# Mamba scan in a metaformer block: a chunk's skip added by TensorE and written by ScalarE instead of VectorE

## The chip, the cores and the metric

One core of a Trainium2 chip runs the whole program. The metric is the device time of one execution in microseconds (us); less is better.

## The reference, cut to what matters

Two metaformer blocks on `x` of 4 samples, 256 channels, 1024 positions. The first block's mixer is a Mamba layer on four chunks of 64 channels; it is the part that the change touches:

```python
h = exp(dt * A) * h + (dt * x) * B          # 16 states, a scan over 1024 positions
y = sum_s h[s] * C[s]                       # read-out
y = (y + xc * D_param) * silu(z)
ym = einsum('bld,od->blo', y, out_proj_w)   # 128 -> 64 channels
ym = ym + skip_scale * chunks               # the skip: chunks is the layer's scaled input
```

The rest (layer norms, an fp8 linear layer, channel attention, a mixture of 8 experts) is left as it is.

## The kernel before, in words

The program has a front (about 0 to 1165 us: four samples, one after the other, then the last sample's later layers) and a mixture-of-experts part. In the front each sample has a stretch of scans, with 64 steps `i` = 16 states `s` for each of the 4 chunks `c`. Every engine runs its own list of instructions in the order in which the code issues them, and they meet at semaphores. Nothing is planned while it runs, so an instruction that waits holds up all that is behind it on its engine.

What a step does:

- ScalarE, `decay(i)` (L1138): exp of 128x1024, into PSUM banks 0-1 or 2-3, or into SBUF for the steps whose drive comes through TensorE. It waits until scan `i-2` is done. Then come `scale_blocks(i)` (L1160, 2 to 4 small products that prepare the next such "turned" drive) and some small work for the next sample (L869, `first_sum`).
- GpSimd, `drive(i)` (L1246) for the steps that aren't turned, and the read-outs `h * C` of 34 of the 64 steps (`read_out`, L1257, two steps late). At step 39 of a sample it also runs one tiny `first_shift` (L1228), which waits for a tiny VectorE reciprocal (L1310, `first_small`) that stands behind VectorE's read-out of step 37.
- VectorE, `scan(i)` (L1567) and the other 30 read-outs (L1577) from the row of C that TensorE spread into banks 4-5 (`crep`).
- TensorE, `turned_drive` (L477, 8 transposes), `c_row` (the row of C, bf16, into banks 4-5), and `sum_states(i-1)` (adds the product of a step into banks 6-7, `ysum`). Its helper has one line for all matrix products, L474.

At the start of chunk `c` (step 16c+1), the chunk before is closed: VectorE multiplies `ysum` by silu(z) (`gate`, L1605, into YF), TensorE projects YF (`out_proj`) into banks 2-3, which the odd decays use too, and VectorE adds the scaled input and writes the chunk into YM (`skip`, L1610). TensorE's next chunk of sums starts with `direct` (the D_param term, two products), which waits for the gate. ScalarE's decay of the step with s = 3 waits for the skip, as it writes banks 2-3. The last chunk of a sample has a path of its own (L1589, L1597).

```python
if c and s == 3:
    act.wait_ge(ym_done, b * NC + c)          # decay, L1136-1137
```

In chunks 1 to 3 the steps with s = 2, 3 and 4 are read out by GpSimd, those with s = 1 and 5 by VectorE, so banks 4-5 hold no row of C in between.

Of the kernel before, what the change touches and what calls it, by code (L numbers as in the profile page):

```python
# [10 lines left out]
ALU = mybir.AluOpType  # L11
# [3 lines left out]
P = 128  # L15
# [4 lines left out]
NC = 4  # L20
# [117 lines left out]
def build_front(nc, t, out, xm_rows, bc_rows, logits, routing, experts):  # L138
    with ExitStack() as ctx:
# [149 lines left out]

        DECAY_SB = XC[:, 0, :]  # L290
        B_TOK = ffn_w.rearrange("p c o -> p (c o)").rearrange("p (n c k) -> p n c k", n=NB, c=NC)

        def square_tile(c):
            return H[:, c % 2, :]
# [177 lines left out]
        def _(pe):  # L472
            def mm(o, lhsT, rhs, start, stop, **k):
                return nc.tensor.matmul(o, lhsT, rhs, start=start, stop=stop, **k)  # L474
# [288 lines left out]
            def scans(b):  # L763
                pe.wait_ge(sz_done, (b + 1) * NC * NH)
                def read_done(i):
                    if on_pool(i):
                        pe.wait_ge(pool_read, b * pool_reads(NI) + pool_reads(i + 1))
                    else:
                        pe.wait_ge(dve_read, b * dve_reads(NI) + dve_reads(i + 1))

                def c_row(i):
                    c, s = i // NS, i % NS
                    if on_pool(i):
                        return
                    if last_on_dve(i - 1) >= 0:
                        pe.wait_ge(dve_read, b * dve_reads(NI) + dve_reads(i))
                    if on_pool(i - 1) and i - 1 in TOK_AT:
                        pe.wait_ge(tok_copied, b * (NC + 1) + (TOK_AT.index(i - 1) + 2))
                    for h in range(NH):
                        m = mm(psum[:, 4 + h, :], sel[:, s, :], BCS[:, c, h * HL:(h + 1) * HL], True, True)  # L780
                    m.then_inc(crep_ready, 1)

                def dtx_turn(c):

                    i = TOK_AT[c]
                    assert on_pool(i) and not on_pool(i + 1)
                    pe.wait_ge(dtx_done, b * NC + c + 1)
                    pe.wait_ge(dve_read, b * dve_reads(NI) + dve_reads(i))
                    for n in range(NB):
                        m = turn(psum[:, 4 + n // 4, (n % 4) * P:(n % 4 + 1) * P], DTX[:, c, n * P:(n + 1) * P])  # L790
                    m.then_inc(tok_turned, 1)

                def turned_drive(i):
                    c, k = i // NS, i % 2
                    pe.wait_ge(h_ready, b * NI + (i - 1))
                    pe.wait_ge(scaled, b * turned_drives(NI) + turned_drives(i) + 1)
                    for n in range(NB):
                        m = turn(psum[:, 2 * k + n // 4, (n % 4) * P:(n % 4 + 1) * P], scaled_tile(c)[:, n, :])
                    m.then_inc(turned_ready, 1)

                def direct(c):
                    if c:
                        pe.wait_ge(yf_ready, b * NC + c)
                    for h in range(NH):
                        mm(psum[:, 6 + h, :], diag_d[:, :], XC[:, c, h * HL:(h + 1) * HL], True, False,
                           skip_group_check=True)

                def sum_states(i):
                    read_done(i)
                    for h in range(NH):  # L810
                        m = mm(psum[:, 6 + h, :], ident[:, :], PRODUCT[PRODUCT_IN[i]][:, h * HL:(h + 1) * HL], False,
                               i % NS == NS - 1, skip_group_check=True)
                        if i == NI - 1 and h == 0:
                            m.then_inc(ysum_half, 1)
                    m.then_inc(ysum_done, 1)

                def out_proj(c):
                    i = min((c + 1) * NS + 1, NI - 1)
                    pe.wait_ge(h_ready, b * NI + (i + 1))
                    p0 = DM * (c % 2)  # L820
                    for h in range(NH):
                        if c == NC - 1 and h == 0:
                            pe.wait_ge(yf_half, b + 1)
                        else:
                            pe.wait_ge(yf_ready, b * NC + c + 1)
                        m = mm(psum[p0:p0 + DM, 2 + h, :], outp_w[:, :], YF[:, h * HL:(h + 1) * HL], True, True)
                        if c == NC - 1 and h == 0:
                            m.then_inc(op_half, 1)
                    m.then_inc(op_ready, 1)

                pe.wait_ge(bc_spread, b * (3 * NC * 16) + 3 * NC * 16)
                c_row(0)
                direct(0)
                for i in range(1, NI):
                    c = i // NS
                    if i % NS == 1 and c:
                        out_proj(c - 1)
                    if i + 2 < NI and is_turned(i + 2):
                        turned_drive(i + 2)
                    if i in TOK_AT:  # L840
                        dtx_turn(TOK_AT.index(i))
                    c_row(i)
                    if i % NS == 1 and c:
                        direct(c)
                    sum_states(i - 1)
                sum_states(NI - 1)
                pe.wait_ge(dve_read, b * dve_reads(NI) + dve_reads(NI))
                xhat_turn(b + 1, 0)
                out_proj(NC - 1)
                xhat_turn(b + 1, 1)  # L850
                y_turn(b)

# [10 lines left out]
        def _(act):  # L863
# [261 lines left out]
            def scans(b, after):  # L1125
                def decay(i):
                    c, s = i // NS, i % NS
                    if i == 0 and after:
                        act.wait_ge(xmt_done, b * 2)
                    if i == 1 and after:  # L1130
                        act.wait_ge(gate_done, b)
                    if s == 0:
                        act.wait_ge(dt_done, b * NC + c + 1)
                    if i >= 2:
                        act.wait_ge(h_ready, b * NI + (i - 1))
                    if c and s == 3:  # L1136
                        act.wait_ge(ym_done, b * NC + c)
                    nc.scalar.activation(DECAY_SB if is_turned(i) else decays[i % 2], DT[:, c, :], ACT.Exp, scale=a_neg[:, s:s + 1]).then_inc(da_ready, 1)  # L1138

                def dtx_tokens(c):  # L1140
                    act.wait_ge(tok_turned, b * (NC + 1) + (c + 2))
# [24 lines left out]
                for i in range(NI):  # L1166
                    decay(i)
                    if i - 2 == TOK_AT[0]:
                        dtx_tokens(0)
                    scale_blocks(i)  # L1170
                    if i - 2 in TOK_AT[1:]:
                        dtx_tokens(TOK_AT.index(i - 2))
                    if 4 <= i < 8 and after:
                        last_norm(b - 1, (2 * i - 8, 2 * i - 7))
                    n = (i - FIRST_AT) % NB
                    k = (i - FIRST_AT) // NB
                    if k == 0:
                        first_sum(b + 1, n)
                    if k == 1:
                        if n == 0:  # L1180
                            first_mean(b + 1)
                        first_square(b + 1, n)
                    if k == 2 and n == 0:
                        first_std(b + 1)
                    if k == 3:
                        first_norm(b + 1, n)
# [98 lines left out]
        def _(dve):  # L1285
# [264 lines left out]
            def scans(b):  # L1550
# [53 lines left out]
                        dve.wait_ge(op_ready, b * NC + c)  # L1604
                    v.tensor_tensor(halves(YF), ysum, halves(SZ[:, c, :]), ALU.mult).then_inc(yf_ready, 1)  # L1605

                def skip(c):
                    dve.wait_ge(op_ready, b * NC + c + 1)
                    p0 = DM * (c % 2)
                    v.scalar_tensor_tensor(halves(YM[p0:p0 + DM, c // 2, :]), halves(xn[p0:p0 + DM, c // 2, :]),  # L1610
                                           scal[p0:p0 + DM, 0:1], op[p0:p0 + DM, :, :], ALU.mult,
                                           ALU.add).then_inc(ym_done, 1)

                for i in range(NI):
                    c, s = i // NS, i % NS
                    scan(i)
                    if c and s == 1:
                        gate(c - 1)
                    if c and s == 2:
                        skip(c - 1)  # L1620
                    if i:
                        read_out(i - 1)
                    if i == FIRST_AT + 2 * NB + NB // 2:
# [51 lines left out]
            for d in range(CT):  # L1675
# [3 lines left out]
                                 ALU.subtract))  # L1679
            fold(v.tensor_tensor(gate_w[:, :, :], gate_w[:, :, :], psum[:, 2, C:C + E].unsqueeze(1).broadcast_to((P, CT, E)),  # L1680
                                 ALU.subtract))
            assert folds[0] == FOLD_DVE
            for c in range(NC):
                log1p(0, c)
# [5 lines left out]


PREP_EPS, PREP_DVE, PREP_ALL = 6, 11, 11 + 3 + 2 + 6 + 5 + 1
FOLD_NBR, FOLD_WG, FOLD_DVE = 12, 14, 20
FIRST_AT = 18
TOKENS_AT, NEXT_AT, X_AT, LAST_DT_AT = 12, 15, 36, 9

# [496 lines left out]
```

## Time and profile before

| | |
|---|---|
| median of 3 runs | 1836.05 us (1835.17 to 1837.93) |
| the profiled execution's own time | 1832.81 us |
| its span | 1830.9 us |
| busy: TensorE, GpSimd, VectorE, ScalarE | 1564.3, 1074.1, 1158.7, 1002.1 us |

The profile is of one execution. Busy shares are means over stages with different limits: in the scans GpSimd and VectorE are both nearly full, in the expert part TensorE is. Times in the rows are us from the start of the span, unless marked ns.

### The profile page before, as it was taken

To read this page: it belongs to the slowest core of one execution; us is meant where nothing else is said; L and a number is where in the kernel's file an instruction comes from. 1 tells how busy PE (TensorE), PEld (TensorE's weight loads), DVE (VectorE), ACT (ScalarE), POOL (GpSimd) and SP (SyncE) were. 2 spreads that over 40 slices of the span, in tenths; PEclk is the share of its full clock that TensorE was granted. 3 is DMA by queue.
4 is the path that set the end of the run, shared out by engine and by line. 5 is a ranking of instruction groups with operands and counts; after the bars stand their busy time and mean duration, and the time that the engine had idled before them with its cause. 6 is when DMAs were issued, how large, how long until landed. Compare 5 with 4: busy or idle time off the path is not lost. (4 is left out here: it accounts for less than half of the span.)

```text
span 1830.9 us, 22984 instructions
## 1 busy us (share of the span) xinstructions
PE 1564.3 (85%) x6577; PEld 1012.4 (55%) x6578; DVE 1158.7 (63%) x1344; ACT 1002.1 (55%) x1950; POOL 1074.1 (59%) x574
## 2 busy tenths in 40 slices
PE   5589889979888888888898888673599999999997
PEld 2144435644444553443564444452488888888896
DVE  3399998489997579998758999746522222222222
ACT  6768775878874887885687877321122222222222
POOL 0499991279995158999037999300345555455543
PEclk9799999999999999999998999895699999999999
DMA  3356650156762055765026676642022222222222
GB/s 104 99 185 228 221 197 10 50 184 224 241 203 86 1 170 196 248 204 169 2 78 217 195 240 200 247 179 71 25 36 34 37 37 39 35 34 40 34 33 26
DMA packets 78401, 222.43 MB, mean 121 GB/s; under 512 B 12588, under 2 KB 31349, under 8 KB 74966
## 3 DMA queue, kind: packets, MB, share of 16 engines
q1 hardware_dynamic: 62390, 202.54, 32.8%
q0 software_dynamic: 15904, 18.66, 6.6%
q8 instruction: 43, 0.70, 0.2%
q14 instruction: 64, 0.52, 0.1%
HBM read 199.76 MB, written 19.82 MB: 120 GB/s over the span
## 5 line engine op out<-in xcount | busy, mean ns | idle before, releaser
L474 PE MATMUL psum<-HC_sb,ident_sb 128*128 128x512 f32 x768 | 368.4, 606 | 36.1 <-POOL HC_sb L1257 25.5
L1986 ACT ACTIVATE hgt_sb<-psum_moe,b_sb 128x256 f32<-128x256 f32 (+1 forms) x312 | 116.5, 456 | 379.8 <-PE psum_moe L1893 252.0
L474 PE MATMUL psum<-experts_sb 64*128 64x512 f32 (+5 forms) x834 | 258.4, 551 | 70.6 <-DVE HC_sb L1577 18.8
L1893 PE MATMUL psum_moe<-XGT_sb,w1s_sb 128*128 128x256 f32 (+1 forms) x1248 | 254.9, 363 | 0.0
L2138 DVE TENSOR_TENSOR YS_sb<-psum_moe,b_sb 128x256 f32<-128x256 f32 x71 | 30.1, 424 | 352.8 <-PE psum_moe L1893 349.2
L1893 PE MATMUL psum_moe<-experts_sb,hgt_sb 128*128 x1136 | 251.7, 379 | 0.7 <-DVE YS_sb L2138 0.7
L1870 POOL DMA_INDIRECT out<-YS_sb,scat_sb x71 | 128.3, 1806 | 209.5 <-DVE YS_sb L2142 193.1
L1138 ACT ACTIVATE psum<-experts_sb 128x1024 f32<-128x1024 f32 x168 | 186.1, 1108 | 118.2 <-DVE experts_sb L1567 70.5
L474 PEld LDWEIGHTS psum<-HC_sb,ident_sb 128*128 128x128 f32 x768 | 139.8, 191 | 189.3 <-issue 104.6
L1160 ACT ACTIVATE experts_sb<-experts_sb 128x128 f32<-128x128 f32 x704 | 227.7, 388 | 18.4 <-PE psum L477 15.2
L1893 PEld LDWEIGHTS psum_moe<-XGT_sb,w1s_sb 128*128 128x128 f32 x1248 | 219.5, 192 | 25.5
L1893 PEld LDWEIGHTS psum_moe<-experts_sb,hgt_sb 128*128 128x128 f32 x1136 | 215.2, 190 | 30.1 <-issue 1.1
L1567 DVE TENSOR_TENSOR_SCAN experts_sb<-psum,DBX_sb 128x1024 f32<-128x1024 f32 x92 | 209.0, 2278 | 27.4 <-ACT psum L1138 13.7
L474 PEld LDWEIGHTS psum<-experts_sb 64*128 64x128 f32 (+5 forms) x834 | 88.5, 155 | 212.3 <-issue 138.1
L1567 DVE TENSOR_TENSOR_SCAN experts_sb<-experts_sb,psum 128x1024 f32<-128x1024 f32 x88 | 199.9, 2272 | 1.9 <-ACT experts_sb L1138 1.4
L1209 POOL TENSOR_TENSOR experts_sb<-experts_sb 128x1024 f32<-128x1024 f32 x16 | 38.7, 2416 | 261.0 <-DVE XSUM_sb L1453 182.8
L1257 POOL TENSOR_TENSOR HC_sb<-X_XT_sb,experts_sb 128x1024 f32<-128x1024 f32 x76 | 180.0, 2372 | 10.7 <-DVE experts_sb L1567 8.2
L1858 POOL DMA_INDIRECT XG_sb<-xm_rows,tab_sb x71 | 70.7, 996 | 163.6 <-DMA gate_rows<-p21t_sb 142.3
L477 PEld LDWEIGHTS psum<-ident_sb,experts_sb 128*128 128x128 f32 x864 | 96.4, 142 | 103.9 <-ACT experts_sb L1160 49.5
L477 PE MATMUL psum<-ident_sb,experts_sb 128*128 128x128 f32 x864 | 114.8, 278 | 31.7 <-ACT experts_sb L1160 14.6
L474 PE MATMUL psum<-experts_sb,ident_sb 128*128 128x512 f32 x256 | 122.9, 602 | 15.1 <-POOL experts_sb L1257 13.4
L1577 DVE TENSOR_TENSOR HC_sb<-psum,experts_sb 128x1024 f32<-128x1024 f32 x96 | 115.3, 1201 | 2.4 <-PE psum L474 2.2
(298 smaller groups left out, 2381.0 us busy)
## 6 DMA issues: line engine op xcount, KB each, us to landing
X_XT_sb<-bc_rows SPq DMA_DIRECT2D x116, 512.0 KB, 4.1
DA_sb<-bc_rows SPq DMA_DIRECT2D x88, 512.0 KB, 5.2
experts_sb<-bc_rows SPq DMA_DIRECT2D x40, 512.0 KB, 5.4
SQ_sb<-bc_rows SPq DMA_DIRECT2D x40, 512.0 KB, 5.9
T_sb<-bc_rows SPq DMA_DIRECT2D x20, 512.0 KB, 5.5
experts_sb<-w1T SPq DMA_DIRECT2D x8, 1024.0 KB, 19.8
experts_sb<-w2T SPq DMA_DIRECT2D x8, 1024.0 KB, 21.8
X_sb<-x_tok SPq DMA_DIRECT2D x5, 1024.0 KB, 6.9
```

Of the source, the lines that this page charges most:

```text
L474: return nc.tensor.matmul(o, lhsT, rhs, start=start, stop=stop, **k)
L477: return nc.tensor.transpose(o, src, ident[:, :])
L1138: nc.scalar.activation(DECAY_SB if is_turned(i) else decays[i % 2], DT[:, c, :], ACT.Exp, scale=a_neg[:, s:s + 1]).then_inc(da_ready, 1)
L1160: m = nc.scalar.activation(scaled_tile(c)[:, n, :], DTX_TOK[:, n, :], ACT.Copy, scale=B_TOK[:, n, c, j % NS:j % NS + 1])
L1209: nc.gpsimd.tensor_tensor(DT[:, c, :], DTX[:, c, :], log_tile(c), ALU.add).then_inc(dt_done, 1)
L1257: nc.gpsimd.tensor_tensor(PRODUCT[PRODUCT_IN[i]], c_rep(q), STATE[STATE_IN[i]], ALU.mult).then_inc(pool_read, 1)
L1567: v.tensor_tensor_scan(STATE[STATE_IN[i]], decay, drive, 0.0, ALU.mult, ALU.add).then_inc(h_ready, 1)
L1577: v.tensor_tensor(halves(PRODUCT[PRODUCT_IN[i]]), crep, halves(STATE[STATE_IN[i]]), ALU.mult).then_inc(dve_read, 1)
L1858: pool.indirect_dma_start(XG[:, k, :], None, xm_rows, bass.IndirectOffsetOnAxis(ap=TAB[:, tile:tile + 1], axis=0)).then_inc(xg_ready[k], 16)
L1870: pool.indirect_dma_start(out, bass.IndirectOffsetOnAxis(ap=SCAT[:, tile:tile + 1], axis=0), YS[:, tile % 4, :], None, compute_op=ALU.add) ...
L1893: return nc.tensor.matmul(o, lhsT, rhs, start=start, stop=stop, **k)
L1986: m = nc.scalar.activation(HGT[:, k, 4 * h + q, 0:w], psum[:, 2 * h + q // 2, (q % 2) * 2 * P:(q % 2) * 2 * P + w], ACT.Gelu, bias=b1[:, b ...
```

## The change

The scaled input is added on TensorE: a 64-row diagonal `SKIP` (skip_scale on the diagonal, both halves of the partitions) times the chunk's input, accumulated behind the projection. Both go into banks 4-5, in the gap between the read-outs of s = 1 and s = 5, one half (512 positions) at a time: the first after the sum of step 16c+1, the second after the sum of step 16c+2. ScalarE copies the result into YM at s = 5. VectorE's skip is gone, the wait moves from ScalarE's decay (s = 3) to TensorE's row of C (s = 5), and `SKIP` is built once at the start by two small VectorE instructions. The last chunk of a sample is as before.

```diff
@@ c_row
+                    if c and s == 5:
+                        pe.wait_ge(ym_done, b * NC + c)
@@ TensorE, the projection
-                def out_proj(c):
-                    i = min((c + 1) * NS + 1, NI - 1)
-                    pe.wait_ge(h_ready, b * NI + (i + 1))
-                    p0 = DM * (c % 2)
+                def out_proj(c, h):
+                    i, p0 = (c + 1) * NS + 1, DM * (c % 2)
+                    pe.wait_ge(yf_ready, b * NC + c + 1)
+                    pe.wait_ge(dve_read, b * dve_reads(NI) + dve_reads(i + 1))
+                    at = psum[p0:p0 + DM, 4 + h, :]
+                    mm(at, outp_w[:, :], YF[:, h * HL:(h + 1) * HL], True, False)
+                    m = mm(at, SKIP[p0:p0 + DM, :], xn[p0:p0 + DM, c // 2, h * HL:(h + 1) * HL], False, True)
+                    if h:
+                        m.then_inc(op_ready, 1)
@@ TensorE, the loop over steps
-                    if i % NS == 1 and c:
-                        out_proj(c - 1)
                     if i + 2 < NI and is_turned(i + 2):
                         turned_drive(i + 2)
...
                     sum_states(i - 1)
+                    if c and i % NS in (2, 3):
+                        out_proj(c - 1, i % NS - 2)
@@ ScalarE
-                    if c and s == 3:
-                        act.wait_ge(ym_done, b * NC + c)
+                def chunk_out(c):
+                    act.wait_ge(op_ready, b * NC + c + 1)
+                    p0 = DM * (c % 2)
+                    nc.scalar.activation(halves(YM[p0:p0 + DM, c // 2, :]), crep[p0:p0 + DM, :, :], ACT.Copy).then_inc(ym_done, 1)
...
                     scale_blocks(i)
+                    if i >= NS and i % NS == 5:
+                        chunk_out(i // NS - 1)
@@ VectorE
-                def skip(c):
-                    dve.wait_ge(op_ready, b * NC + c + 1)
-                    p0 = DM * (c % 2)
-                    v.scalar_tensor_tensor(halves(YM[p0:p0 + DM, c // 2, :]), halves(xn[p0:p0 + DM, c // 2, :]),
-                                           scal[p0:p0 + DM, 0:1], op[p0:p0 + DM, :, :], ALU.mult,
-                                           ALU.add).then_inc(ym_done, 1)
...
-                    if c and s == 2:
-                        skip(c - 1)
@@ VectorE, once at the start
+            fold(v.tensor_tensor(SKIP, ident[:, 0:DM], ident[:, DM:P], ALU.add))
+            fold(v.tensor_scalar(SKIP, SKIP, scal[:, 0:1], None, ALU.mult))
```

## Rows read from the trace of the kernel before

**Rows 1.** The page: groups by line; the line VectorE's skip has.

```profile
L1610 DVE SCALAR_TENSOR_TENSOR T_sb<-experts_sb,scal_sb,psum 64x1024 f32<-64x1024 f32 x12 | 15.1, 1259 | 0.1
```

**Rows 2.** Who waited for whom, ScalarE: us in total, times, longest.

```profile
ACT psum L1138 <- DVE T_sb L1610: 46.9, 8, 6.3
```

**Rows 3.** Busy time by stretch (PE, PEld, DVE, ACT, POOL; clock, DMA share), second sample.

```profile
433.90:481.10 47.20, 42.25 (x140) 19.75 (x140) 44.71 (x25) 39.76 (x97) 46.24 (x21) 1.00 0.65 213
481.10:531.85 50.75, 42.54 (x142) 19.93 (x142) 46.33 (x27) 39.16 (x76) 47.84 (x25) 1.00 0.65 221
```

**Rows 4.** GpSimd in order of time: start, duration, then idle time before it.

```profile
437.51 2.36 POOL L1257 TENSOR_TENSOR experts_sb<-X_XT_sb,experts_sb 128x1024 f32<-128x1024 f32 x1 [0.82 <-DVE experts_sb L1567]
...
456.25 2.36 POOL L1257 TENSOR_TENSOR experts_sb<-X_XT_sb,experts_sb 128x1024 f32<-128x1024 f32 x1
...
490.86 2.36 POOL L1257 TENSOR_TENSOR HC_sb<-X_XT_sb,experts_sb 128x1024 f32<-128x1024 f32 x1 [1.19 <-DVE experts_sb L1567]
...
498.71 0.21 POOL L1228 TENSOR_TENSOR experts_sb<-experts_sb 128x8 f32<-128x8 f32 x1 [0.84 <-DVE experts_sb L1310]
...
554.70 2.39 POOL L1257 TENSOR_TENSOR HC_sb<-X_XT_sb,experts_sb 128x1024 f32<-128x1024 f32 x1
```

**Rows 5.** GpSimd's waits in chunk 2 of the first sample (189.1 to 240.1).

```profile
POOL HC_sb L1257 <- DVE experts_sb L1567: 2.1, 2, 1.5
POOL experts_sb L1228 <- DVE experts_sb L1310: 1.2, 1, 1.2
```

**Rows 6.** The same of the fourth sample (1067.7 to 1118.4).

```profile
POOL HC_sb L1257 <- DVE experts_sb L1567: 2.0, 2, 1.3
```

**Rows 7.** TensorE's products in order of time, start of chunk 1, second sample.

```profile
435.24 4.16 PE L474 MATMUL psum<-experts_sb 128*64 128x512 f32 x10 [1.42 <-DVE experts_sb L1605]
...
440.95 1.04 PE L477 MATMUL psum<-ident_sb,experts_sb 128*128 128x128 f32 x8
441.82 1.88 PE L474 MATMUL psum<-HC_sb,ident_sb 128*128 128x512 f32 x4
443.54 1.88 PE L474 MATMUL psum<-experts_sb,ident_sb 128*128 128x512 f32 x4
```

**Rows 8.** TensorE's weight loads: the front's start (64-row tiles), then chunk 1.

```profile
43.37 0.19 PEld L474 LDWEIGHTS psum<-experts_sb 64*128 64x128 f32 x2 [0.24 <-issue]
...
436.12 0.14 PEld L474 LDWEIGHTS psum<-experts_sb 128*64 128x64 f32 x1 [0.29 <-issue]
437.07 0.64 PEld L474 LDWEIGHTS psum<-experts_sb 128*128 128x128 bf16 x4 [0.81 <-issue]
```

**Rows 9.** ScalarE in order of time, chunk 1 of the second sample.

```profile
445.81 0.40 ACT L869 ACTIVATE X_sb<-X_sb 128x256 f32<-128x256 f32 x1
...
446.21 1.13 ACT L1138 ACTIVATE experts_sb<-experts_sb 128x1024 f32<-128x1024 f32 x1
```

**Rows 10.** One line's instructions: ScalarE's copy of PSUM into SBUF (min/median/max ns).

```profile
L1144 ACT ACTIVATE experts_sb<-psum x16: 1024/1024/1025, 97.8 to 1105.7; 128x1024 f32<-128x1024 f32 x16
```

**Rows 11.** VectorE in order of time, around the three chunk starts of the second sample.

```profile
433.89 1.20 DVE L1605 TENSOR_TENSOR experts_sb<-psum,experts_sb 128x1024 f32<-128x1024 f32 x1
...
447.47 2.29 DVE L1567 TENSOR_TENSOR_SCAN experts_sb<-experts_sb,psum 128x1024 f32<-128x1024 f32 x1 [0.35 <-ACT experts_sb L1138]
...
452.98 2.26 DVE L1567 TENSOR_TENSOR_SCAN experts_sb<-psum,experts_sb 128x1024 f32<-128x1024 f32 x1
...
481.13 1.22 DVE L1605 TENSOR_TENSOR experts_sb<-psum,experts_sb 128x1024 f32<-128x1024 f32 x1
...
495.12 2.29 DVE L1567 TENSOR_TENSOR_SCAN experts_sb<-experts_sb,psum 128x1024 f32<-128x1024 f32 x1
...
531.85 1.22 DVE L1605 TENSOR_TENSOR experts_sb<-psum,experts_sb 128x1024 f32<-128x1024 f32 x1 [0.48 <-PE psum L474]
...
544.68 2.29 DVE L1567 TENSOR_TENSOR_SCAN experts_sb<-experts_sb,psum 128x1024 f32<-128x1024 f32 x1
```

**Rows 12.** GpSimd's first drive in the order of time.

```profile
83.28 4.64 POOL L1246 TENSOR_TENSOR DBX_sb<-DA_sb,experts_sb 128x1024 f32<-128x1024 f32 x2 [17.96 <-DMA DA_sb<-bc_rows]
```

More of the change, by code:

```diff
@@ L291, in build_front @@
         B_TOK = ffn_w.rearrange("p c o -> p (c o)").rearrange("p (n c k) -> p n c k", n=NB, c=NC)
+        SKIP = FB[:, 0:DM]
         def square_tile(c):
@@ L815, in sum_states, with last_out_proj @@
                     m.then_inc(ysum_done, 1)
-                def out_proj(c):
-                    i = min((c + 1) * NS + 1, NI - 1)
-                    pe.wait_ge(h_ready, b * NI + (i + 1))
-                    p0 = DM * (c % 2)
+                def out_proj(c, h):
+                    i, p0 = (c + 1) * NS + 1, DM * (c % 2)
+                    assert not on_pool(i) and all(on_pool(i + k) for k in (1, 2, 3)) and not on_pool(i + 4)
+                    pe.wait_ge(yf_ready, b * NC + c + 1)
[5 more added lines that the diff above has]
+                        m.then_inc(op_ready, 1)
+                def last_out_proj():
+                    c, p0 = NC - 1, DM * ((NC - 1) % 2)
+                    pe.wait_ge(h_ready, b * NI + NI)
                     for h in range(NH):
-                        if c == NC - 1 and h == 0:
+                        if h == 0:
                             pe.wait_ge(yf_half, b + 1)
@@ L825, in out_proj @@
                             pe.wait_ge(yf_ready, b * NC + c + 1)
[L826 to L829, printed above, removed]
+                        mm(psum[p0:p0 + DM, 2 + h, :], outp_w[:, :], YF[:, h * HL:(h + 1) * HL], True,
+                           True).then_inc(op_ready if h else op_half, 1)
                 pe.wait_ge(bc_spread, b * (3 * NC * 16) + 3 * NC * 16)
@@ L848, in scans @@
                 xhat_turn(b + 1, 0)
-                out_proj(NC - 1)
+                last_out_proj()
                 xhat_turn(b + 1, 1)
@@ L1692 @@
 PREP_EPS, PREP_DVE, PREP_ALL = 6, 11, 11 + 3 + 2 + 6 + 5 + 1
-FOLD_NBR, FOLD_WG, FOLD_DVE = 12, 14, 20
+FOLD_NBR, FOLD_WG, FOLD_DVE = 12, 14, 22
 FIRST_AT = 18
```

## The prediction, made before the changed kernel ran

> **What bounds the kernel now.** I read the busy time by stretch first, then each engine in order of time around the three places per sample where a chunk is closed, then the waits. In the scans of the second sample GpSimd is busy 46.24 of 47.20 us in chunk 1 and 47.84 of 50.75 us in chunk 2, at TensorE's full clock (granted 1.00, the 2.4 GHz level) [rows 3]. So GpSimd sets the pace of chunks 1 to 3; VectorE is late only near a chunk's start. GpSimd's idle time there has names: 0.82 us for scan 18, and in chunk 2 1.19 us for scan 35 and 0.84 us for VectorE's tiny reciprocal [rows 4]; in the first sample the last two are 1.5 and 1.2 us, in the fourth 1.3 us and again the 0.8 us [rows 5, 6]. What happens to VectorE's or ScalarE's time counts only as far as it moves these GpSimd instructions.
>
> The removed pieces: VectorE's skip, 12 times 1.26 us, 15.1 us [rows 1]; ScalarE's waits for it, 46.9 us in the eight of its waits whose decay goes to PSUM [rows 2]. Neither is a gain as it stands.
>
> **What the skip's removal could give.** If nothing new is late, decay 35 runs early, scan 35 follows VectorE's read-out of step 33 at once, and GpSimd's two idle times of chunk 2 close: 2.7 us in the first sample (1.5 + 1.2), 2.0 in the second (1.19 + 0.84), 2.1 in the fourth (1.3 + 0.8), and as much in the third by the same pattern, 9 us in all. In chunk 1 nothing: the 0.82 us stands ahead of the skip, and after it GpSimd is full. In chunk 3 nothing either.
>
> **What the new chain costs.** Count from g, the gate's start; a wait that moves to step s = 5 is only harmless if the copy is ready by then. TensorE works in order, and by row the prices are: four passes of 512 columns (the two products of a state's sum) 1.72 us (441.82 to 443.54), a turned drive 0.87 us (440.95 to 441.82), the last pass's tail 0.16 us (1.88 less 1.72), the first product after the gate at g + 1.35 (435.24 less 433.89) [rows 7, 11]. In the new order there stand behind the gate:
> direct 1.72, the sum of s = 0 1.72, the turned drive of s = 4 0.87, the sum of s = 1 1.72, first half of the projection 1.72 (projection and skip, two passes each), the sum of s = 2 1.72, second half 1.72. With 1.35 that is g + 12.54. After the 64-column passes the next weights stand at 437.07, where 436.12 + 2 x 0.43 is 436.98 [rows 8]: 0.09 per change, 0.18 for two. With the tail: the result is there at g + 12.9. Its inputs are not later than this queue: VectorE's read-out of s = 1 is over near g + 4.4, GpSimd's of s = 2 at 437.51 + 2.36, g + 6.0 [rows 4].
>
> The new products are the skip's, 64 rows by 64 columns, which the trace doesn't show. From below they cost 0 (if they ran beside the projection), by the nearest row, the 128x64 passes, 0.43 us a pass as for full ones [rows 8]; from above I allow the same and 0.25 to 0.5 us more per half for changing shapes twice. I take 0.43 us: time goes by the 512 columns, in all rows.
>
> At this place a rule of the Trainium skill is worth weighing. The row first: on 64-row tiles two weight loads fall into one slot of 0.43 us in the front's start (x2, 0.19 + 0.24 idle) [rows 8], so pairs on disjoint tiles do overlap. The Trainium skill, "TensorEngine Tiling (Array Packing)", Theoretical Speedup, gives up to 2x for a small dimension, and Key Properties says that a change of mode drains the array. By the first the skip's products would be free, by the second both halves dearer. Here projection and skip share their 64 columns and the projection takes all rows, so I expect no overlap.
>
> ScalarE reaches the copy (after decay and scale blocks of s = 5) before that: by my walk through its list near g + 10, and surely before g + 12.3, where decay 22 stood in the old order (446.21) [rows 9]. So it waits about 3 us for TensorE, and the decay of s = 6 is behind it. The copy takes 1.02 us by the PSUM copy of the same length [rows 10]; 64 partitions instead of 128 change nothing I would count on.
>
> *Chunk 1.* Copy g + 12.95, a first_sum behind it (0.40, 445.81 to 446.21), decay 22 from g + 14.3 to g + 15.45 (1.13) [rows 9], scan 22 at g + 15.5. Before: g + 13.58 (447.47). It is 1.9 us later although it had waited for the skip before. From scan 22 VectorE is full up to scan 24 (452.98 less 447.47 is two scans of 2.19 and a read-out of 1.12), so scan 24 starts at g + 21.0 and ends at g + 23.2 [rows 11]. GpSimd's read-out 24 stood at 456.25, g + 22.36, with 1.0 us to spare [rows 4]; it becomes g + 23.3: **+0.9**. Later scans have more to spare.
>
> *Chunk 2.* No first_sum stands here: decay 38 g + 13.95 to g + 15.1, scan 38 at g + 15.1; before at 495.12, g + 13.99 [rows 11]. Its read-out 37, the reciprocal and GpSimd's first_shift follow it without a gap, and GpSimd is idle there already: **+1.1**. The 1.19 us before read-out 35 is gained, and lost again at first_shift. In the first sample both idle times are 0.3 us longer [rows 5], scan 38 is that much later already, and I take +0.8.
>
> *Chunk 3.* Decay 54 at the same g + 13.95, scan 54 at g + 15.1, before 544.68 less 531.85, g + 12.83: 2.2 later [rows 11]. VectorE's scan 56 ends 7.7 us later (three scans, a read-out), g + 22.8; GpSimd's read-out 56 stood at 554.70, g + 22.85 [rows 4]: **0 to +0.1**. The wait is paid from VectorE's slack.
>
> **Edits at nothing.** The two small instructions that build SKIP delay VectorE by some tenths at the start; GpSimd's first drive waits 17.96 us for a DMA there, long after its own work [rows 12]. Without that cover 0.4 us once. TensorE's wait for ym_done before the row of C of s = 5: the copy ends at g + 14, and what is behind it (that row, then the sum of s = 4, which needs GpSimd's product) is wanted only when VectorE has ended the scan of s = 6, g + 17.7. Clearing banks 2-3 for the odd decays gives ScalarE an early decay 19, 35 and 51, which is what exposes the later wait. DMA queues see no new or moved issue; their waits follow GpSimd.
>
> **Sum.** First sample 0.9 + 0.8 = 1.7, the other three 2.0 each plus up to 0.1: 7.7 to 8, I say **+8 us**. On the profiled execution (1830.9 span, 1.9 around it) that is 1840.8; the median of the runs stands 3.2 above that execution, so 1836.05 + 8 = **1844 us**.
>
> **Rivals.**
> 1. The result is ready when ScalarE comes (TensorE's queue is shorter than I make it): GpSimd's idle times of chunk 2 close, -9, 1827 us. For it: the old skip was a wait of over 5 us. Against: seven items of TensorE in a row, each with a measured price, and back-to-back rows. It would need g + 10. Chance 0.12.
> 2. The skip's products overlap with others or cost nearly nothing: the result comes 1.72 earlier, at g + 11.2. Chunk 1: scan 22 +0.2, inside the spare time, 0. Chunk 2: scan 38 0.6 earlier, and so is first_shift, 0.9 in the first sample. -2.7, 1833.4 us, no change to be told. The case of the first rule above. Chance 0.13.
> 3. Forecast, 1844 us: TensorE's queue makes the copy late, the copy holds decay s = 6, that holds VectorE, that holds GpSimd. Decides from about g + 11.8 on (sum zero). Chance 0.60.
> 4. Changes of tile shape drain: 0.25 to 0.5 us more per half, 0.5 to 1 us on all three places, chunk 3 without spare time now: 12 x 0.5 to 12 x 1, 1850 to 1856 us. Chance 0.12. The case of the second rule.
>
> The remaining 0.03 is for VectorE being the bound after all, up to the 15 us of the skip.
>
> **How the numbers follow.** What can be told from no change is 0.2%, 3.7 us. Faster: rival 1 and a little of the rest, 0.15; same: rival 2, and the forecast half-sized, 0.14; slower: 0.71. The range reaches from below rival 2 to the cheaper end of rival 4: 1831 to 1851; outside are rival 1 and the dear end of 4. The forecast's own range is 1840 to 1848.
>
> **What would show it.** ScalarE's new copy idle about 3 us before each of 12, released by TensorE; VectorE idle 4 to 4.6 us before the scans 22, 38 and 54, released by ScalarE's decay; these scans at g + 15.5, 15.1, 15.1; the projection's end at g + 12.9; GpSimd without idle time at read-out 35 but with 3 us at first_shift. Wrong would be: the copy not waiting, the products under 1.72 us per half, or scan 22 at less than g + 14.5.

## The result and the profile after

The changed kernel takes 1849.93 us (median of 4 runs, 1848.79 to 1851.0) against 1836.74 us for the kernel before (4 runs): ratio 1.0075, 95% interval 1.0061 to 1.0089. That is slower, by 13.2 us (11 to 16). The forecast was 1844 us in a range of 1831 to 1851: the direction and the way it happens held, the size was 8 us against 13.

The two profiled executions are further apart, 1848.1 against 1830.9 us of span: the one of the kernel before was 3.9 us faster than that kernel's median, the one of the changed kernel stood at its own. In what follows "gate + x" is x us after the start of VectorE's gate of that chunk. Busy time by stretch says where: here chunk 1, chunk 2 and chunk 3 (up to the last chunk's own path) of the second sample, with the columns of [rows 3].

```profile
437.28:486.25 48.97, 44.34 (x145) 20.04 (x144) 43.04 (x24) 40.92 (x98) 46.27 (x21) 1.00 0.58 207
486.25:538.84 52.59, 44.99 (x147) 20.13 (x146) 44.82 (x27) 40.66 (x78) 47.75 (x25) 1.00 0.62 213
538.84:584.80 45.96, 41.57 (x127) 18.15 (x126) 38.95 (x22) 25.42 (x49) 41.45 (x18) 1.00 0.49 166
```

The stretches were 47.20 and 50.75 us [rows 3], and the third:

```profile
531.85:577.04 45.19, 39.05 (x123) 18.13 (x124) 40.49 (x23) 24.92 (x48) 41.46 (x18) 1.00 0.51 171
```

So +1.8, +1.8 and +0.8 us, at an unchanged clock and with GpSimd's busy time unchanged to 0.1 us. GpSimd has only become idle for longer. VectorE is 1.5 to 1.7 us less busy per chunk and the stretch is longer all the same. The other samples show much the same (first: +1.7, +1.5, +0.7). Four samples give 17 us, as far as the two profiled executions are apart.

GpSimd in order of time (start, duration, idle before), after; against [rows 4]:

```profile
455.72 2.36 POOL L1276 TENSOR_TENSOR HC_sb<-X_XT_sb,experts_sb 128x1024 f32<-128x1024 f32 x1 [0.92 <-DVE experts_sb L1586]
...
461.36 2.36 POOL L1276 TENSOR_TENSOR experts_sb<-X_XT_sb,experts_sb 128x1024 f32<-128x1024 f32 x1 [0.97 <-DVE experts_sb L1586]
...
494.60 2.35 POOL L1276 TENSOR_TENSOR HC_sb<-X_XT_sb,experts_sb 128x1024 f32<-128x1024 f32 x1
...
505.68 0.20 POOL L1247 TENSOR_TENSOR experts_sb<-experts_sb 128x8 f32<-128x8 f32 x1 [4.11 <-DVE experts_sb L1329]
...
562.48 2.36 POOL L1276 TENSOR_TENSOR HC_sb<-X_XT_sb,experts_sb 128x1024 f32<-128x1024 f32 x1 [0.76 <-DVE experts_sb L1586]
```

Read-outs 22 and 24 now wait for VectorE (24 is at gate + 24.1, it was at + 22.4). Read-out 35 has lost its idle time, as the removed skip promised. But first_shift waits 4.11 us where it waited 0.84, and read-out 56 of chunk 3, which had nothing to spare, waits 0.76.

VectorE, after; against [rows 11] (L1624 is the gate):

```profile
437.28 1.19 DVE L1624 TENSOR_TENSOR experts_sb<-psum,experts_sb 128x1024 f32<-128x1024 f32 x1
...
446.08 2.26 DVE L1586 TENSOR_TENSOR_SCAN experts_sb<-psum,DBX_sb 128x1024 f32<-128x1024 f32 x1
453.35 2.29 DVE L1586 TENSOR_TENSOR_SCAN experts_sb<-experts_sb,psum 128x1024 f32<-128x1024 f32 x1 [5.01 <-ACT experts_sb L1150]
...
461.05 1.20 DVE L1596 TENSOR_TENSOR HC_sb<-psum,experts_sb 128x1024 f32<-128x1024 f32 x1
...
502.09 2.29 DVE L1586 TENSOR_TENSOR_SCAN experts_sb<-experts_sb,psum 128x1024 f32<-128x1024 f32 x1 [4.75 <-ACT experts_sb L1150]
...
554.54 2.29 DVE L1586 TENSOR_TENSOR_SCAN experts_sb<-experts_sb,psum 128x1024 f32<-128x1024 f32 x1 [4.36 <-ACT experts_sb L1150]
```

Scans 22, 38 and 54 start at gate + 16.1, + 15.8 and + 15.7, each released by ScalarE's decay. Up to scan 21 VectorE is ahead of the kernel before by 2.1 us (+ 8.8 against + 10.9); then it loses more than that in one wait. ScalarE and who held it:

```profile
450.78 1.02 ACT L1155 ACTIVATE T_sb<-psum 64x1024 f32<-64x1024 f32 x1 [3.75 <-PE psum L477]
451.70 0.40 ACT L883 ACTIVATE X_sb<-X_sb 128x256 f32<-128x256 f32 x1
...
452.10 1.14 ACT L1150 ACTIVATE experts_sb<-experts_sb 128x1024 f32<-128x1024 f32 x1
```

```profile
ACT T_sb L1155 <- PE psum L477: 48.2, 12, 4.2
```

All twelve copies wait for TensorE, about 4 us each, 48.2 us in all. In the kernel before, ScalarE waited twelve times for the skip too: the eight waits of [rows 2], 46.9 us, and four of chunk 2, where a table load stands ahead of the decay and has a row of its own:

```profile
ACT L1138 <- DVE T_sb L1610: 15.1, 4, 3.9
```

That is 62.0 us before and 48.2 after. The wait is a quarter shorter, but it has been moved to where the next turned step needs ScalarE, and there it costs. TensorE's queue, weight loads and products:

```profile
444.75 0.19 PEld L477 LDWEIGHTS psum<-experts_sb 128*64 128x64 f32 x2 [0.76 <-issue]
445.75 0.19 PEld L477 LDWEIGHTS psum<-experts_sb 64*64 64x64 f32 x2 [0.81 <-issue]
446.75 0.30 PEld L477 LDWEIGHTS psum<-experts_sb,ident_sb 128*128 128x128 f32 x2 [0.81 <-issue]
...
448.67 0.19 PEld L477 LDWEIGHTS psum<-experts_sb 128*64 128x64 f32 x2 [0.76 <-issue]
449.67 0.19 PEld L477 LDWEIGHTS psum<-experts_sb 64*64 64x64 f32 x2 [0.81 <-issue]
```

```profile
438.53 1.98 PE L477 MATMUL psum<-experts_sb 128*128 128x512 f32 x4 [0.89 <-DVE experts_sb L1624]
440.35 1.88 PE L477 MATMUL psum<-HC_sb,ident_sb 128*128 128x512 f32 x4
442.07 1.04 PE L480 MATMUL psum<-ident_sb,experts_sb 128*128 128x128 f32 x8
442.94 1.88 PE L477 MATMUL psum<-HC_sb,ident_sb 128*128 128x512 f32 x4
```

The queue is the one forecast, item by item: direct at + 1.25, the sum of s = 0 at + 3.1, the turned drive at + 4.8, the sum of s = 1 at + 5.7, the halves at + 7.5 and + 11.4. Two passes of the projection take from 444.75 to 445.75, two of the skip to 446.75, the sum to 448.67. Without a change of tile shape these would be 0.86, 0.86 and 1.72: the changes in these three stretches add 0.14, 0.14 and 0.20 us, as the weight load no longer runs ahead of the passes before it (0.76 to 0.81 us idle instead of 0.24). From the sum of s = 1 (442.94, gate + 5.66) to the last product (449.67, gate + 12.39) 14 passes take 6.73 us, where 14 x 0.43 is 6.02: the five changes together add 0.71 us.

### The profile page after: what moved, and what is told of

It reads as the page before. It is cut to its first block and busy times, and to the rows that moved or that the text cites. A ratio compares the mean times of both kernels' runs of the same rounds, so it can differ in the third digit from the quotient of the medians.

```text
span 1848.1 us, 23085 instructions
## 1 busy us (share of the span) xinstructions
PE 1589.7 (86%) x6625; PEld 1012.6 (55%) x6626; DVE 1140.4 (62%) x1334; ACT 1014.0 (55%) x1962; POOL 1076.7 (58%) x574
## 5 line engine op out<-in xcount | busy, mean ns | idle before, releaser
L477 PE MATMUL psum<-HC_sb,ident_sb 128*128 128x512 f32 x768 | 372.8, 611 | 35.2 <-POOL HC_sb L1276 18.3
L477 PE MATMUL psum<-experts_sb 64*128 64x512 f32 (+6 forms) x882 | 287.9, 555 | 67.8 <-DVE HC_sb L1596 22.7
L477 PEld LDWEIGHTS psum<-experts_sb 64*128 64x128 f32 (+6 forms) x882 | 90.9, 152 | 230.9 <-issue 138.2
L480 PEld LDWEIGHTS psum<-ident_sb,experts_sb 128*128 128x128 f32 x864 | 96.0, 141 | 100.5 <-ACT experts_sb L1177 40.4
L480 PE MATMUL psum<-ident_sb,experts_sb 128*128 128x128 f32 x864 | 114.1, 277 | 28.7 <-DVE experts_sb L1586 13.7
```

Of the source, the lines that this page charges most:

```text
L480: return nc.tensor.transpose(o, src, ident[:, :])
```

## The experiments

The runs outside the scans vary by a few us from one execution to the next, so each verdict rests on the stretches of the second sample too (chunk 1 and 2 from gate to gate, chunk 3 up to the last chunk's own path). Of "theory" below: TensorE's result is late, and the wait goes over ScalarE and VectorE to GpSimd. The kernel before had a median of 1835.2 to 1835.4 us beside these runs.

| kernel | median us | ratio to before, 95% interval | chunk 1 / 2 / 3, us |
|---|---|---|---|
| before | 1836.74 (beside the change) | | 47.2 / 50.7 / 45.2 |
| the change | 1849.93 | 1.0075 (1.0061, 1.0089) | 49.0 / 52.6 / 46.0 |
| copy_later | 1837.85 | 1.0014 (1.0001, 1.0026) | 47.4 / 51.3 / 45.2 |
| halves_together | 1836.51 | 1.0009 (1.0, 1.0018) | 47.3 / 51.1 / 45.1 |
| no_skip_product | 1832.65 | 0.9986 (0.9977, 0.9995) | 47.4 / 50.6 / 45.1 |
| later_together | 1838.01 | 1.0013 (1.0005, 1.0022) | 47.3 / 51.2 / 45.1 |
| full_rows | 1849.1 | 1.0072 (1.0059, 1.0085) | 48.7 / 52.3 / 45.7 |
| short_copy | 1846.68 | 1.0066 (1.005, 1.0082) | 48.1 / 51.7 / 45.2 |
| before_recip_early | 1830.94 | 0.9983 (0.9971, 0.9996) | 47.3 / 49.8 / 45.2 |
| after_recip_early | 1837.75 | 1.0011 (1.0003, 1.002) | 49.0 / 49.2 / 46.0 |
| spread | 1832.2 | 0.9981 (0.9969, 0.9994) | 47.0 / 49.6 / 45.2 |
| halves_recip_early | 1824.83 | 0.9945 (0.9931, 0.9958) | 47.3 / 48.4 / 45.2 |
| spread_recip_early | 1821.23 | 0.9925 (0.9911, 0.9939) | 47.0 / 48.4 / 45.2 |

**Does the wait cost, or the work?** copy_later only moves the copy:

```diff
                     decay(i)
+                    if i >= NS and i % NS == 6:
+                        chunk_out(i // NS - 1)
...
-                    if i >= NS and i % NS == 5:
-                        chunk_out(i // NS - 1)
```

> The changed kernel with ScalarE's copy moved one decay later: behind decay of s = 6 instead of ahead of it. Theory (the copy waits for TensorE's result at gate + 13.4 and holds decay s = 6, and so scans 22, 38 and 54, and through them GpSimd): scan s = 6 at gate + 11 to 11.5 instead of + 16, the copy still begins at + 13.4 to 13.5, VectorE now waits under 2.5 us for the row of C of s = 5, first_shift about 1 us earlier than in the kernel before: some 4 us under the kernel before, 1832. Rival A (the copy's 1 us of ScalarE work is the price, wherever it stands): no change against the changed kernel, 1850. Rival B (TensorE's added products and shape changes slow the state sums, which hold GpSimd): 1848 to 1850.

The same work, 12 us less than the change: rivals A and B fall as the whole cause. But the median missed the forecast 1832 by 6 us, and chunks 1 and 2 are 0.2 and 0.6 us longer than in the kernel before. Scan 22 did not start at + 11; it started at gate + 14.5 (gate at 433.50), released by TensorE's transposes (L480) and no longer by ScalarE:

```profile
448.03 2.29 DVE L1586 TENSOR_TENSOR_SCAN experts_sb<-experts_sb,psum 128x1024 f32<-128x1024 f32 x1 [3.46 <-PE psum L480]
```

halves_together removes no work either:

```diff
-                    if c and i % NS in (2, 3):
-                        out_proj(c - 1, i % NS - 2)
+                    if c and i % NS == 2:
+                        out_proj(c - 1, 0)
+                        out_proj(c - 1, 1)
```

> The changed kernel with both halves of the projection behind the sum of s = 1, the sum of s = 2 after them. TensorE's work is the same, the result is there some 1.9 us earlier, gate + 11.5. Theory: scan s = 6 at gate + 14.1 (chunk 1) and + 13.9 (chunk 2), against + 13.6 and + 14.0 in the kernel before, so GpSimd loses nothing in chunk 1 and 2: about the kernel before, 1834 to 1839. Rival A: 1850. Rival B: 1850 or more.

The median is as forecast: a result 2 us earlier wins nearly all of the loss back. The scans come a little later than forecast, at gate + 14.4 for + 14.1 and + 13.9, and here too TensorE's transposes release scan 22 (gate at 435.02). ScalarE's decay 22 is over at 449.07, 0.3 us earlier:

```profile
449.40 2.29 DVE L1587 TENSOR_TENSOR_SCAN experts_sb<-experts_sb,psum 128x1024 f32<-128x1024 f32 x1 [3.31 <-PE psum L480]
```

no_skip_product takes the work away:

```diff
-                    mm(at, outp_w[:, :], YF[:, h * HL:(h + 1) * HL], True, False)
-                    m = mm(at, SKIP[p0:p0 + DM, :], xn[p0:p0 + DM, c // 2, h * HL:(h + 1) * HL], False, True)
+                    m = mm(at, outp_w[:, :], YF[:, h * HL:(h + 1) * HL], True, True)
```

> Leaves out the product that adds the scaled input in chunks 0 to 2 (the output lacks it); projection, copy, waits and order as in the changed kernel. It takes two passes and one change of tile shape, 1.0 us, from each half. Theory: result at gate + 11.5, the same times as halves_together, 1834 to 1839. Rival A: 1850, since the copy is there. Rival B: 1836 to 1840 too, as TensorE's added work is gone; it differs from the theory in halves_together only.

The stretches are those of the theory (scan 38 at gate + 13.8, forecast + 13.9); the median is 1 us under the range. Here ScalarE's decay releases the scan, as in the change. Order and work thus buy nearly the same, scan 22 at gate + 14.4 and + 14.1, though what holds it last differs: the queue up to the transposes in the one, the result and the copy in the other.

**The second wait under the first.** later_together has both edits.

> Both edits at once: the copy behind decay s = 6, both halves behind the sum of s = 1. Theory: nothing is late any more: scan s = 6 at gate + 11, row of C of s = 5 ready near + 13.2, when VectorE has just ended that scan; GpSimd's idle time before read-out 35 and first_shift closes: 9 us under the kernel before, 1827 to 1829. Rival A: 1850 less little. Rival B: 1845 to 1850.

A miss by 9 us: no faster than either edit alone. VectorE of this kernel, second sample (gate at 435.93), then TensorE:

```profile
450.30 2.29 DVE L1587 TENSOR_TENSOR_SCAN experts_sb<-experts_sb,psum 128x1024 f32<-128x1024 f32 x1 [3.31 <-PE psum L480]
```

```profile
447.41 1.98 PE L477 MATMUL psum<-experts_sb,ident_sb 128*128 128x512 f32 x4
449.23 1.04 PE L480 MATMUL psum<-ident_sb,experts_sb 128*128 128x128 f32 x8
```

Scan 22 is a turned step, and its drive (the eight transposes at 449.23) stands in TensorE's queue behind both halves and the sum of s = 2. With ScalarE free, the same queue holds VectorE directly. It already did in halves_together, where the scan stood at the same gate + 14.37, so moving the copy could add nothing. I had followed the queue only to the projection's end and not to the next turned drive. Here rival B was right in part: the added work counts, for what stands behind it.

**The price of the tile shape and of the copy.** full_rows:

```diff
-        SKIP = FB[:, 0:DM]
+        SKIP = FB[:, 0:P]
...
-                    m = mm(at, SKIP[p0:p0 + DM, :], xn[p0:p0 + DM, c // 2, h * HL:(h + 1) * HL], False, True)
+                    m = mm(at, SKIP[:, p0:p0 + DM], xn[:, c // 2, h * HL:(h + 1) * HL], False, True)
...
-            fold(v.tensor_tensor(SKIP, ident[:, 0:DM], ident[:, DM:P], ALU.add))
+            fold(v.tensor_copy(SKIP, ident[:, :]))
```

> The changed kernel with the diagonal as 128 rows by 64 columns (zeros in the other half's rows, multiplied with the other chunk's input), so the projection and the skip have the same tile shape; the same passes, the same columns, one change of shape less per half. Theory (TensorE's queue sets the copy, a change of shape costs 0.14 us there): result 0.28 us earlier at each of the 12 places, which have no spare time: 3 us less, 1845 to 1848. If the 64 rows themselves cost nothing and changes cost nothing: 1850. If the 64-row passes had been cheaper than full ones: over 1850.

Its weight loads (second sample) show a half of 1.86 us, 445.77 to 447.63, where the change has 2.00:

```profile
445.77 0.19 PEld L477 LDWEIGHTS psum<-experts_sb 128*64 128x64 f32 x2 [0.76 <-issue]
446.25 0.14 PEld L477 LDWEIGHTS psum<-experts_sb 128*64 128x64 f32 x1 [0.29 <-issue]
446.68 0.14 PEld L477 LDWEIGHTS psum<-experts_sb 128*64 128x64 f32 x1 [0.29 <-issue]
447.63 0.30 PEld L477 LDWEIGHTS psum<-experts_sb,ident_sb 128*128 128x128 f32 x2 [0.81 <-issue]
```

Scans 22, 38 and 54 start 0.28 us earlier, and each stretch is 0.3 us shorter, 3.5 us over twelve: a later result is paid one for one. The median moved by only 0.8 us and missed its forecast (1849.1 for 1845 to 1848); the profiled execution is 0.5 us shorter, so the rest of it is 3 us longer, which is not explained. 64 rows are no cheaper than 128, and one change of shape costs 0.14 us. Then short_copy:

```diff
-                    nc.scalar.activation(halves(YM[p0:p0 + DM, c // 2, :]), crep[p0:p0 + DM, :, :], ACT.Copy).then_inc(ym_done, 1)
+                    nc.scalar.activation(halves(YM[p0:p0 + DM, c // 2, :])[:, :, 0:4], crep[p0:p0 + DM, :, 0:4], ACT.Copy).then_inc(ym_done, 1)
```

> The changed kernel with ScalarE's copy cut to 8 of 1024 columns (YM is left unwritten for the rest): the wait for TensorE stays, 0.8 us of the copy's own time goes. Theory: scan s = 6 at gate + 15.2 instead of + 16, so 0.8 us less at each of 12 places: 1840 to 1842. Rival A (the copy's work is the whole price): 1835 to 1836. Rival C (the copy is hidden and the wait alone counts): 1850.

The copy went from 1.02 to 0.17 us and the stretches fell by the same 0.8 to 0.9 us, 10 us over twelve. The median fell by 3.2 only, a miss (1846.7 for 1840 to 1842). The rest of this kernel's execution is longer, with runs from 1843 to 1852; it works on a YM that is mostly not written, and what makes it longer was not looked into. By the stretches the copy's work is 0.9 us of the path each time, not the whole price.

**Is GpSimd the bound?** One line moves VectorE's tiny reciprocal one step ahead, in the kernel before and in the changed one:

```diff
-                    if i == FIRST_AT + 2 * NB + NB // 2:
+                    if i == FIRST_AT + 2 * NB + NB // 2 - 1:
                         first_small(b + 1)
```

> The kernel before with VectorE's tiny reciprocal (first_small) one step earlier, behind scan 37 instead of behind read-out 37. Theory (GpSimd is the bound in chunk 2, so that its idle time before first_shift is end-to-end time): 0.84 us, 1.2 in the first sample, less: 3 to 4 us under the kernel before. Rival D (VectorE is the bound in chunk 2): no change.

> The changed kernel with the same one-step move. Theory: of the late scan 38 GpSimd then sees only its read-out 38, not first_shift: read-out 38 near gate + 18.1 instead of + 21.9, 3.5 to 3.8 us less per sample, 1835 to 1838; the losses of chunk 1 (1.7) and chunk 3 (0.8) stay. Rival D: 1850.

The gains are 4.4 us for the 3 to 4 forecast, and the changed kernel stands at 1837.75, inside its range: chunk 2 is 0.9 us shorter in the kernel before, 3.4 us in the changed one. That makes GpSimd the bound in chunk 2; for chunks 1 and 3 no such run was made, and it is read from the rows. GpSimd of after_recip_early, chunk 2 (gate 483.96):

```profile
499.16 0.20 POOL L1247 TENSOR_TENSOR experts_sb<-experts_sb 128x8 f32<-128x8 f32 x1
499.33 2.35 POOL L1265 TENSOR_TENSOR DBX_sb<-SQ_sb,experts_sb 128x1024 f32<-128x1024 f32 x1
502.16 2.36 POOL L1276 TENSOR_TENSOR HC_sb<-X_XT_sb,experts_sb 128x1024 f32<-128x1024 f32 x1 [0.48 <-DVE experts_sb L1586]
```

Scan 38 is as late as in the change (gate + 15.84), and nearly all of it is hidden. Chunk 2's whole loss went through an instruction of 0.2 us: with the move on both sides the stretch is 49.2 us after the change and 49.8 before it. What is left of the change, 1837.75 against 1830.94 us, comes with the losses of chunks 1 and 3, +1.7 and +0.8 us a sample, less the 0.6 us of chunk 2.

**The order that lets the change gain.** spread puts each half behind the turned drive that VectorE needs first (and keeps the copy of copy_later):

```diff
                     if i + 2 < NI and is_turned(i + 2):
                         turned_drive(i + 2)
+                    if c and s in (2, 4):
+                        out_proj(c - 1, s // 2 - 1)
...
-                    c_row(i)
+                    if not (c and s == 5):
+                        c_row(i)
...
+                    if c and s == 3:
+                        continue
+                    if c and s == 4:
+                        sum_states(i - 2)
+                        c_row(i + 1)
                     sum_states(i - 1)
```

> The changed kernel with TensorE's order changed so that the turned drives of s = 4 and s = 6 stand ahead of a half of the projection each (first half behind the turned drive of s = 4, second behind that of s = 6, then the sum of s = 2, the row of C of s = 5 and the sum of s = 3), and the copy behind decay s = 6. Theory (what holds VectorE is the turned drive of s = 6 and the row of C of s = 5 behind TensorE's queue): scan s = 6 at gate + 11, its read-out near + 14.8, first_shift near + 16.1 against + 17.6 in the kernel before: 4 to 6 us under the kernel before, 1829 to 1832. Rival B (TensorE's added 2.2 us per half cost the same in any order): as later_together, 1838.

> spread with the reciprocal one step earlier. Theory: GpSimd has no idle time left in chunk 2 but the 0.7 us before read-out 34: 2.0 us per sample, 2.7 in the first, 9 us under the kernel before, 1825 to 1828. Rival D (VectorE bounds): as spread.

> halves_together with the reciprocal one step earlier. Scan 38 stays near gate + 14, which GpSimd now meets only at read-out 38 (about + 18): 1 to 2 us less per sample than halves_together, 1827 to 1831; if chunk 1 loses more than it gains, 1834.

spread: scan 38 at gate + 11.0, its read-out at + 15.0, first_shift at + 16.4; 3 us under the kernel before, 0.2 us above the range. Rival B falls. spread_recip_early is the fastest, 14 us under the kernel before and 29 under the change, and 4 us under its range:

```profile
430.57:477.58 47.01, 43.76 (x143) 20.42 (x144) 43.30 (x25) 40.82 (x98) 46.21 (x21) 1.00 0.64 215
477.58:526.00 48.42, 44.13 (x144) 20.59 (x146) 44.70 (x27) 40.38 (x78) 47.71 (x25) 1.00 0.67 232
```

GpSimd is busy 47.71 of 48.42 us: the 0.7 us left is the one before read-out 34. That is 2.5 us per sample against the kernel before, 10 to 11 in all, and the two profiled executions are 9.5 us apart; the medians say 14, and the difference is not explained. Part of the gain is the reciprocal's alone: before_recip_early has it without the change and stands at 1830.94. Against it the change in this order gains 10 us by the medians, 7 by the stretches. halves_recip_early came to 1824.83, 10.5 us under the kernel before and 2 us under its range.

## Why the prediction was right in its way and short in its size

- *GpSimd is the bound, the removed skip is worth nothing by itself.* Right; shown by the two recip kernels for chunk 2, and for chunks 1 and 3 by [rows 3] against the stretches after. VectorE's 15 us are gone and the kernel is slower.
- *What the removal could give, 2.0 us per sample in chunk 2.* Half shown: read-out 35's idle time closed in the change, but first_shift's idle time did not close in any order by the removal alone. spread shortens chunk 2 by 1.1 us, with 1.18 us idle left before first_shift, where VectorE's read-out waits 1.76 us for the row of C; the 2.3 us of spread_recip_early need the moved reciprocal too, which alone gives 0.9.
- *The new chain on TensorE.* The items, their order, the 0.43 us a pass for 64 rows and ScalarE's wait held. Up to the sum of s = 1 the queue is on the forecast's time, gate + 5.66 in both. Mis-sized was the term "0.09 per change, 0.18 for two": from there to the last product are five changes, 0.71 us. So the copy began at + 13.5, not + 12.95. I had counted two of five, and the 0.09 is only the wait until the next weights are loaded; that load, hidden otherwise, then stands in the open as well (the load at 446.75 and the next, at 447.29, are 0.54 us apart, not 0.43).
- *Three places without spare time.* The 0.55 us arrived in full, and a little more: scans 22, 38, 54 at + 16.1, + 15.8, + 15.7 against + 15.5, + 15.1, + 15.1. Chunk 1 lost 1.8 for a forecast 0.9, chunk 2 1.8 for 1.1, chunk 3 0.8 for 0 to 0.1. In chunk 1 I had also let GpSimd start 0.1 us after VectorE's scan 24; after, VectorE goes on at 461.05 and the read-out starts at 461.36, 0.3 later, and in chunk 3 it is the same (562.23 and 562.48). So 4.4 us per sample for 2.0. Of the missing 2.4 us the changes of tile shape, rival 4's cause, are 3 x 0.53 = 1.6, on top of the forecast's own mechanism; about 0.4 is GpSimd's later start, and the rest are steps of 0.1 us along the chain. That the time still lies in the range owes something to the range's width: it ends 1 us above the result, at the cheap end of rival 4. No row stood behind rival 4's 0.25 to 0.5 us per half; what was missing, 0.53 us for both halves, is its lower end.
- *Rivals 1 and 2.* The result never was ready when ScalarE came, and the skip's products did not overlap: 1.00 us per two passes.
- *Edits at nothing.* The start (first scan at 86.6 us, 86.8 before) and the row of C held.

The Trainium skill, "TensorEngine Tiling (Array Packing)", has two rules for this place. The trace agrees with the one under Key Properties, that a change of mode drains the array, at 0.14 to 0.20 us each; the 2x of Theoretical Speedup is not seen here, where both products use the same 64 columns.

## What to carry to other kernels

Work taken off an engine that isn't the bound buys nothing; a wait moved with it is paid where it lands, so follow each in-order queue past the new instruction to the next thing that any other engine takes from it, not only to the result of the change. Put new TensorE work behind what VectorE needs next, and a wait behind what others need from the waiting engine. And look for tiny instructions that sit behind long ones and feed the bounding engine: here one moved line was worth 4 us in the kernel before and 12 in the changed one. Such a gain is not the change's own: compare each order with the kernel before that has the same line moved.

## What the runs showed of the hardware

- A change of tile shape (128x128, 128x64, 64x64) between matmuls costs 0.14 to 0.20 us, 0.71 us for five of them: the next weights are loaded only after the last pass (0.76 to 0.81 us idle instead of 0.24).
- An fp32 pass of 512 columns takes 0.43 us with 64 or 128 rows and 64 or 128 columns alike (two passes and a change 1.00 us for 128x64 and for 64x64 tiles), when nothing runs beside it.
- ScalarE's copy out of PSUM takes 1.02 us for 64 partitions and for 128.
